# Recurrence sums by accumulating DMAs in place of adds, with three buffers and per-step preparation

## The reference

```
tf    = sigmoid(sum(cond))                       # per batch
decay = exp(-exp(w)) * (0.5 + 0.5 * tf)          # per batch and channel
ek, ekv = exp(min(k, 30)), exp(min(k, 30)) * v   # v = k here
nf, df = forward scans of a = a*decay + ekv, b = b*decay + ek     # over time
nb, db = the same scans backwards
euk = exp(min(u + k, 30))
num = nf + nb - ekv + euk * v
den = df + db - ek + euk
gate = sigmoid(x) * num / max(den, 1e-8) * (0.8 + 0.2 * tf)
```

## Time and profile before

| | |
|---|---|
| median of 3 runs | 501.41 us (500.61 to 501.68) |
| span of the profiled execution | 502.5 us |
| VectorE busy | 336.9 us, 67% |
| TensorE busy | 286.8 us, 57% |
| ScalarE busy | 186.0 us, 37% |
| GpSimd busy | 135.9 us, 27% |
| share of the chain that ended last | VectorE 38%, TensorE 34%, issue 9%, GpSimd 8%, ScalarE 8% |
| data moved by DMA | 7.53 MB |

### The profile page before, as it was taken

The page is one execution under the profiler, slowest core; times in us unless marked ns, Lnnn a source line. Parts: engine busy times, 40 slices in busy tenths (PEclk is TensorE's granted clock), DMA queues, the critical chain, the costliest instruction groups (busy, mean ns, idle before and its releaser), DMA issues.

```text
span 502.5 us, 5307 instructions
## 1 busy us (share of the span) xinstructions
PE 286.8 (57%) x1958; PEld 179.4 (36%) x1958; DVE 336.9 (67%) x533; ACT 186.0 (37%) x272; POOL 135.9 (27%) x122
## 2 busy tenths in 40 slices
PE   0031055325475525237245776889899999964753
PEld 0021032112233213113123335576677777732532
DVE  1998999798979889999446665424443533069553
ACT  6521153733463432344132213252463442325322
POOL 2545452565435462654510210200100000000000
PEclk9999999976556677656666876886956575596887
DMA  7000000000002000000400000000000000000010
GB/s 239 1 0 1 0 0 1 1 0 2 0 1 85 0 0 1 0 0 1 168 1 0 0 1 0 1 1 2 0 1 1 2 0 1 1 0 1 22 42 21
DMA packets 4056, 7.53 MB, mean 15 GB/s; under 512 B 1088, under 2 KB 2496, under 8 KB 3648
## 3 DMA queue, kind: packets, MB, share of 16 engines
q1 hardware_dynamic: 4032, 7.21, 4.2%
HBM read 6.16 MB, written 1.05 MB: 14 GB/s over the span
## 4 chain that ended last, share of the span: by engine, by line
DVE 38%; PE 34%; issue 9%; POOL 8%; ACT 8%; DMA 1%; SPq 1%; DVEq 0%; ACTq 0%; POOLq 0%
PE PS L1107 9%; DVE db L627 6%; PE PM L1056 5%; PE PO L1124 4%; DVE df L627 3%; DVE nb L627 3%; PE PM L953 3%; DVE nf L627 3%; DVE rsum L695 3%; POOL df L281 3%; PE PM L1005 3%; POOL df L282 3%; DVE EU L863 2%; PE PO L988 2%; ACT E L467 2%
## 5 line engine op out<-in xcount | busy, mean ns | idle before, releaser
L797 DVE TENSOR_REDUCE kp<-PS 128x2 f32<-128x256 f32 x64 | 32.2, 553 | 37.6 <-PE PS L1087 37.5
L980 PE MATMUL PO<-E,vt 128*32 128x256 f32 x256 | 30.6, 626 | 38.4 <-DVE ytok L722 24.8
L988 PE MATMUL PO<-ident,yc 128*128 128x128 f32 x64 | 20.3, 416 | 56.3 <-ACT yc L452 56.3
L385 ACT ACTIVATE df<-df,lnmin 128x512 f32<-128x512 f32 x16 | 11.5, 720 | 101.3 <-POOL df L282 101.3
L538 ACT ACTIVATE E<-PS 128x384 f32<-128x384 f32 x64 | 29.7, 491 | 46.2 <-PE PS L1107 45.5
L467 ACT ACTIVATE E<-PS,negc,escale 128x1024 f32<-128x1024 f32 x32 | 38.3, 1197 | 22.6 <-PE PS L967 22.6
L695 DVE TENSOR_REDUCE rsum<-E 128x4 f32<-128x1024 f32 x32 | 38.1, 1207 | 1.4 <-ACT E L467 1.4
L281 POOL TENSOR_TENSOR df<-df,db 128x512 f32<-128x512 f32 x16 | 24.9, 1557 | 51.7 <-DVE nb L627 51.6
L279 POOL TENSOR_TENSOR mv<-EU,vf 128x512 f32<-128x512 f32 x12 | 25.0, 2082 | 42.7 <-DVE EU L617 42.7
L627 DVE TENSOR_TENSOR_SCAN db<-DT,ek 128x512 f32<-128x512 f32 x16 | 34.5, 2158 | 0.0
L941 PE MATMUL PM<-w,sg 128*128 128x256 f32 x32 | 14.7, 637 | 33.2 <-DVE sg L637 33.2
(11 more groups left out here) (160 smaller groups left out, 652.1 us busy)
## 6 DMA issues: line engine op xcount, KB each, us to landing
kT<-in_kT SPq DMA_DIRECT2D x4, 256.0 KB, 4.3
xT<-in_xT SPq DMA_DIRECT2D x4, 256.0 KB, 5.9
G<-in_attn SPq DMA_DIRECT2D x1, 1024.0 KB, 4.9
ek<-in_w SPq DMA_DIRECT2D x1, 1024.0 KB, 4.9
ekv<-in_w SPq DMA_DIRECT2D x1, 1024.0 KB, 7.0
out<-G SPq DMA_DIRECT2D x8, 128.0 KB, 1.7
w<-in_attn SPq DMA_DIRECT2D x1, 512.0 KB, 7.1
cond<-in_cond SPq DMA_DIRECT2D x1, 128.0 KB, 4.4
```

Source lines behind the costliest of these rows:

```text
L797: nc.vector.tensor_reduce(kp[:, b % 2, u * H + 2 * j:u * H + 2 * j + 2, D], PS[:, at0:at0 + 2, lo:hi], AX, ALU.max, negate=True).then_inc( ...
L980: ins = nc.tensor.matmul(PO[SLOT * g:SLOT * (g + 1), q % 2, 0:T], vt[:, b % 2, v * H + 4 * c + g, :], E[:, (2 * q + g // 2) % 4, g % 2, v ...
L988: ins = nc.tensor.transpose(PO[:, q % 2, T + u * P:T + (u + 1) * P], yc[:, q % 2, u * P:(u + 1) * P], ident[:])
```

## The change

VectorE's four scans write to `fwd[r]` and `bwd[r]`, each a tile of two rows of 512 (denominator and numerator side by side), the two forward scans first. ScalarE writes exp(u+k) of one step to `mid[r][0]`, VectorE turns it into m there, GpSimd writes m*v to `mid[r][1]`. Two DMAs on GpSimd's queue with `accum_op=ALU.add` then add 128 x 1,024 floats each: `mid` onto `fwd` when the forward scans are done, and, when that has landed and the backward scans are done, `bwd` onto `fwd`. GpSimd waits for the first; the second's landing is waited for by ScalarE. The adds L281, L282, L284, L285, L597 and L599 go. The rings have three places.

`eu(l)` and `decay_wide(l)` become `prepare(n)`: two exponentials of 256 columns and one copy of 2 x 255 decays per step, the segment borders being zeroed once at the start. `prepare(n+1)` stands behind the reciprocal of step n. Tiles that the second half of the program borrowed from the old buffers are moved to others.

```diff
-        RING = 2
-        mv = sb("mv", [P, RING, SEG])
-        nf = sb("nf", [P, RING, SEG])
...
+        RING = 3
+        DT = [sb(f"DT{i}", [P, SEG + 8]) for i in range(2)]
+        mid = sb("mid", [P, RING, 2, SEG])
+        fwd = sb("fwd", [P, RING, 2, SEG])
+        bwd = sb("bwd", [P, RING, 2, SEG])
...
 # GpSimd
             def wkv(n):
                 l, b, r = wkv_at(n)
-                m = EU[l % 2][:, seg(b)]
+                turns = 16 * (n // RING + 1)
                 pool.wait_ge(S["m_done"], n + 1)
-                if n >= RING:
-                    pool.wait_ge(S["gate_ready"], n + 1 - RING)
-                if n < B:
-                    nc.gpsimd.tensor_tensor(mv[:, r], m, vf[:, seg(b)], ALU.mult).then_inc(S["mv_done"], 1)
-                else:
-                    link(nc.gpsimd.tensor_tensor(mv[:, r], m, vf[:, seg(b)], ALU.mult))
-                pool.wait_ge(S["scan_done"], 4 * (n + 1))
-                link(nc.gpsimd.tensor_tensor(df[:, r], df[:, r], db[:, r], ALU.add))
-                nc.gpsimd.tensor_tensor(df[:, r], df[:, r], m, ALU.add).then_inc(S["den_ready"], 1)
-                if n >= B:
-                    link(nc.gpsimd.tensor_tensor(nf[:, r], nf[:, r], nb[:, r], ALU.add))
-                    nc.gpsimd.tensor_tensor(nf[:, r], nf[:, r], mv[:, r], ALU.add).then_inc(S["num_ready"], 1)
+                nc.gpsimd.tensor_tensor(mid[:, r, 1], mid[:, r, 0], vf[:, seg(b)], ALU.mult).then_inc(S["mv_done"], 1)
+                pool.wait_ge(S["mv_done"], n + 1)
+                pool.wait_ge(S["scan_done"], 4 * n + 2)
+                nc.gpsimd.dma_start(fwd[:, r], mid[:, r], accum_op=ALU.add).then_inc(S[f"mid_added{r}"], 16)
+                pool.wait_ge(S[f"mid_added{r}"], turns)
+                pool.wait_ge(S["scan_done"], 4 * n + 4)
+                nc.gpsimd.dma_start(fwd[:, r], bwd[:, r], accum_op=ALU.add).then_inc(S[f"back_added{r}"], 16)
...
 # ScalarE
-            def eu(l):
-                if l >= 2:
-                    act.wait_ge(S["den_ready"], B * (l - 1))
+            def prepare(n):
+
+                l, b, r = wkv_at(n)
+                if n >= RING:
+                    act.wait_ge(S[f"mid_added{r}"], 16 * (n // RING))
                 for h in range(HALF):
-                    nc.scalar.activation(halves(EU[l % 2])[:, :, h, :], halves(kT)[:, :, h, :], ACT.Exp,
-                                         bias=vec[:, 1, l, h:h + 1]).then_inc(S["eu_done"], 1)
+                    nc.scalar.activation(mid[:, r, 0, h * T:(h + 1) * T], kT[:, seg(b, h * T, T)], ACT.Exp,
+                                         bias=vec[:, 1, l, h:h + 1]).then_inc(S["prep_done"], 1)
+                if n == 0:
+                    act.wait_ge(S["decay_ready"], 1 + LAYERS)
+                if n >= 2:
+                    act.wait_ge(S["scan_done"], 4 * (n - 1))
+                nc.scalar.activation(DT[n % 2][:, 0:SEG].rearrange("p (h t) -> p h t", t=T)[:, :, 1:T],
+                                     dec[:, l, b, :, None].broadcast_to([P, HALF, T - 1]),
+                                     ACT.Copy).then_inc(S["prep_done"], 1)
...
                 if 2 <= p < B * PAIRS + 2 and wkv_slot(p - 2) >= 0:
                     wkv(wkv_step(p - 2))
+                    if wkv_step(p - 2) + 1 < LAYERS * B:
+                        prepare(wkv_step(p - 2) + 1)
...
-                if p == 5:
-                    eu(2)
-                if p == 12:
-                    decay_wide(3)
-                if p == 14:
-                    eu(3)
...
 # VectorE
             def gate(n):
-                if n < B:
-                    link(nc.vector.tensor_tensor(nf[:, r], nf[:, r], nb[:, r], ALU.add))
-                    dve.wait_ge(S["mv_done"], n + 1)
-                    link(nc.vector.tensor_tensor(nf[:, r], nf[:, r], mv[:, r], ALU.add))
-                else:
-                    dve.wait_ge(S["num_ready"], n + 1 - B)
                 dve.wait_ge(S["rec_done"], n + 1)
...
-                dve.wait_ge(S["eu_done"], HALF * (l + 1))
+                dve.wait_ge(S["prep_done"], 3 * (n + 1))
...
+                for i, src in enumerate((ek, ekv)):
+                    nc.vector.tensor_tensor_scan(fwd[:, r, i], ahead, src[:, seg(b)], 0.0, ALU.mult,
+                                                 ALU.add).then_inc(S["scan_done"], 1)
+                for i, src in enumerate((ek, ekv)):
+                    nc.vector.tensor_tensor_scan(bwd[:, r, i][:, ::-1], behind, src[:, seg(b)][:, ::-1], 0.0, ALU.mult,
+                                                 ALU.add).then_inc(S["scan_done"], 1)
```

More of the change, by code:

```diff
@@ L87, in build @@
         G = [sb(f"G{l}", [P, N]) for l in range(LAYERS)]
-        EU = [sb(f"EU{i}", [P, N]) for i in range(2)]
-        DT = [sb(f"DT{i}", [P, N + 8]) for i in range(2)]
-        RING = 2
-        mv = sb("mv", [P, RING, SEG])
-        nf = sb("nf", [P, RING, SEG])
-        nb = sb("nb", [P, RING, SEG])
-        df = sb("df", [P, RING, SEG])
-        db = sb("db", [P, RING, SEG])
+        RING = 3
[3 more added lines that the diff above has]
+        bwd = sb("bwd", [P, RING, 2, SEG])
+        halfs = sb("halfs", [P, 2 * CH * T])
         vec = sb("vec", [P, 2, LAYERS, HALF])
@@ L170, in build @@
         x3tok = [G[2][:, i * SEG:(i + 1) * SEG].rearrange("p (u c) -> p u c", u=TT) for i in range(B)]
[L171 to L173 removed]
+        xrnd = [fwd[:, 0, i, :].rearrange("p (u c) -> p u c", u=TT) for i in range(2)]
+        xqb = [mid[:, 0, i, 0:SEG // 2].bitcast(BF16).rearrange("p (u c) -> p u c", u=TT) for i in range(2)]
+        xqT = [bwd[:, 0, i // 2, (i % 2) * SEG // 2:(i % 2 + 1) * SEG // 2].bitcast(BF16)
                .rearrange("p (u k t) -> p u k t", u=TT, k=HALF) for i in range(B)]
[L175 to L176 removed]
+        hrelu = [fwd[:, 1 + i].rearrange("p n c -> p (n c)") for i in range(2)]
+        hsq = [bwd[:, 1 + i].rearrange("p n c -> p (n c)") for i in range(2)]
         hqb = [kT[:, i * HID // 2:(i + 1) * HID // 2].bitcast(BF16) for i in range(2)]
@@ L297, in _ @@
             nc.gpsimd.memset(epsc[:], EPS_RMS).then_inc(S["pads_set"], 1)
+            for i in range(2):
+                nc.gpsimd.memset(DT[i][:, 0:SEG + 1:T], 0.0).then_inc(S["decay_edge"], 1)
             pool.wait_ge(S["cond_tanh"], 1)
@@ L310, in _ @@
             wkv(1)
-            decay_zero(1)
             wkv(2)
@@ L389, in decay_wide @@
[L389 to L395, removed]
+                nc.scalar.activation(fwd[:, r, 0], fwd[:, r, 0], ACT.Exp, scale=-1.0).then_inc(S["rec_done"], 1)
@@ L406, in _ @@
                     nc.scalar.activation(cth[:], csum[:], ACT.Tanh, scale=0.5).then_inc(S["cond_tanh"], 1)
-            decay_wide(0)
-            eu(0)
+            act.wait_ge(S["decay_edge"], 2)
+            prepare(0)
+            prepare(1)
             for b in range(B):
@@ L412, in _ @@
             act.wait_ge(S["ln_bias"], 1)
+            prepare(2)
             wkv(0)
-            decay_wide(1)
-            eu(1)
+            prepare(3)
             def rms(b):
@@ L458, in _ @@
             kT_copy(0)
+            prepare(4)
             for p in range(SLOTS0):
@@ L620, in wkv @@
                     dve.wait_ge(S["gate_ready"], n + 1 - RING)
-                dve.wait_ge(S["decay_tile"], l + 1)
                 dve.wait_ge(S["ekv_done"], b + 1)
-                fwd = DT[l % 2][:, seg(b)]
-                bwd = DT[l % 2][:, seg(b, 1)][:, ::-1]
-                for out, src, back in ((df, ek, False), (db, ek, True), (nf, ekv, False), (nb, ekv, True)):
-                    s = src[:, seg(b)]
-                    nc.vector.tensor_tensor_scan(out[:, r][:, ::-1] if back else out[:, r], bwd if back else fwd,
-                                                 s[:, ::-1] if back else s, 0.0, ALU.mult,
+                ahead = DT[n % 2][:, 0:SEG]
+                behind = DT[n % 2][:, 1:SEG + 1][:, ::-1]
+                for i, src in enumerate((ek, ekv)):
[3 more added lines that the diff above has]
+                    nc.vector.tensor_tensor_scan(bwd[:, r, i][:, ::-1], behind, src[:, seg(b)][:, ::-1], 0.0, ALU.mult,
                                                  ALU.add).then_inc(S["scan_done"], 1)
```

39 lines of the change are left out of this document (15 added, 24 removed).

## The result

The changed kernel takes 559.95 us (median of 4 runs, 557.99 to 561.94), the kernel before 501.01 (median of 4, the three runs given above and one more). The ratio is 1.1165, 95% interval 1.1102 to 1.1227: 59 us slower. The forecast was 550, in a range of 504 to 590.

What follows compares the result with a forecast made beforehand. Bound: ScalarE's in-order stream waiting for the denominator, in the first half. Terms 44.0 - 1.5 + 9.9 - 10.8 + 3.2 + 4.0 = +48.8 on 501.4 gave 550 us, range 504 to 590.

Steps and rivals of the forecast that it cites:

- The signs that were named: Sums near 14 us after L617 starts; L385 waiting over 10 us for a DMA; L617 intervals 21.7, 23.9 and 16.2.
- slot 0: First of eight slots in a recurrence period; steps stand at slots 0, 3 and 6; its L617 interval forecast at 16.2 us.
- The unknown, L = 4.9: One accumulating DMA from issue to landing, 4.9 us, taken from the 1,024 KB load row; 3.6 to 6.2 got 0.60.
- a plain copy's price: Rival: each DMA lands in 3.1 us like a plain 512 KB; sum about +3, 504 us; chance 0.13.
- prepare, 1.1 us on the path: ScalarE's two exponentials and decay copy for the next step, behind the denominator: 1.1 us per step.
- the third kind: Intervals from slot 6 to the next slot 0: 12.9 us of VectorE's own work before, 16.2 forecast.
- by columns a quarter: Sizing of ScalarE's per-step preparation: a quarter of a layer's cost, 1.0 us, taken as 1.1 with a third instruction.
- The eight intervals, +42.5: Steps 4 to 15, slots 0 to 3 and 3 to 6: 5.5 us more each, 44.0, less 1.5 for layer 0's adds.
- the three, +9.9: Steps 4 to 15, slot 6 to next 0: L617 after 16.2 us against 12.9, 3.3 us more each.
- The first four steps, -10.8: Start to step 4: earlier start, gates without two adds, L613 unslowed (-0.9); step 4 at 52.6, not 63.38.
- The tail: Step 15 to the last gate: gate starts 15.05 us after L617 instead of 11.84, +3.2.
- the shared queues: Two 1,024 KB weight loads beside the last two accumulates, +3; the attention weights' load once, +1.

Runs made afterwards that it cites:

- the kernel with adds: Changed kernel with its two DMAs taken out and the four adds of a step given back to GpSimd, `prepare` still behind the reciprocal: 514.55 us, ratio 1.025.
- the last kernel: Denominator by GpSimd adds, numerator by DMAs, `prepare` ahead, GpSimd's multiply moved behind the denominator's adds, numerator's scans first: 480.89 us, ratio 0.9574 of the kernel before.

## Why the prediction was right

- **What bounds the kernel.** Right: ScalarE's in-order stream behind the denominator, not VectorE's load. VectorE has 25 us less work and the kernel takes 59 us more; taking 1.6 us off each landing gave 39.6 back. The signs that were named came: sums at m+13.9, the steps of slot 0 released by the decay copy L369, intervals of 22.2 and 24.2 for the 21.7 and 23.9 forecast.
- **The unknown, L = 4.9, by the bytes read.** Measured 4.5 from the issue's record, and 0.5 us from the release to that record, so 5.0 in the sum. The choice of the row with as many bytes read came within 0.4 us, and the copy's 2.9 shows that it mattered: with a plain copy's price I would have said 504. That the bytes read are the reason isn't shown. The row was a load from outside SBUF on another queue, so some luck is in how near it came. The prediction put GpSimd's issue inside L, and there it is.
- **prepare, 1.1 us on the path.** Measured 1.35 to 1.4 in each interval; 11.7 us in all in the kernel with adds, and beside the DMAs it chained the third kind to the landing. With it ahead of the reciprocal, the third kind is 6 us shorter. Mis-sized by 0.3 us per step, the term "by columns a quarter": two short exponentials take 0.89 us together.
- **The eight intervals, +42.5; the three, +9.9.** Measured +46.8 and +13.8. The difference is 0.2 us of sums and 0.3 of preparation for each, and the kernel before took 12.3 us in the mean of the third kind, not 12.9, which I had read off one of three. The one landing beside the attention weights took 5.3 us for 4.5, near the +1 forecast for it.
- **The first four steps, -10.8.** Measured -8.7. From L597 at 28.32 to the end of L604 at 32.31 is 4.0 us, not 3.9, which changes little. Step 0 started at 10.03, not 9.5, the k load having landed a microsecond later; the memset started at 38.38 instead of 37.5 and took 2.13 us; and L613 of step 3 was still slowed, by the v rows and not by an add, so its -0.9 didn't come.
- **The tail.** +3.2 and +3 for the shared queues; measured +8.1. The collision was foreseen and costed 1.6 us low: the last landing grew by 4.1 us and the one before by 0.5.
- **The sum.** +48.8 forecast, +60.0 to the last gate, +58.9 in the medians. Each term had its sign. All were off the same way, most by a few tenths, eleven times over, so nothing cancelled.
- **What I didn't say.** The DMAs have a real gain, 8.0 us in the first four steps, and 12.2 us to the last gate where the numerator alone uses them (232.3 against 244.5 with adds). The prediction booked it under dropped adds, as a gain of VectorE's; with the adds given to GpSimd instead, step 4 comes 0.7 us sooner than before, though step 0 starts 2.1 us sooner.

## What to carry to other kernels

Before a sum is moved to a DMA, ask who waits for it and how long after: a landing of 3 to 5 us is free where the consumer comes 7 to 15 us later, as the gate did here, and costs its whole length in every round where an in-order engine stands behind it. Split the work by that, put whatever an engine can do while it waits ahead of the wait in its stream, and keep GpSimd's two-input instructions away from VectorE's, reductions excepted. A change that removes busy time from the busiest engine and lengthens a chain of waits has to be judged by the chain.

## What the runs showed of the hardware

- An accumulating DMA from GpSimd inside SBUF, 128 rows: 4.5 us for 512 KB, 3.3 for 256 KB; a plain one 2.9 for 512 KB. The issue holds GpSimd 0.87 us (copy 0.59), and its record starts 0.5 us after the scan that releases it, where a GpSimd add starts 0.13 after.
- Two loads of 1,024 KB beside it stretch a landing from 4.56 to 8.65 us, and the landing of the second load from 6.9 to 10.0.
- A VectorE instruction with two SBUF inputs beside a GpSimd one with two took 1.0 us longer in each case here: a scan 2.22 for 1.2, the product ekv 1.64 for 0.69, one of 128 columns 1.31 for 0.29. Of instructions with one input, TENSOR_SCALAR was slowed alike (ek 1.37 for 0.43) and the row sums were not, beside the same adds (1.17 to 1.22). The Trainium skill (SBUF — State Buffer, section Who interferes with whom) names such pairs as contending; these are the amounts. The records look like taking turns: in step 15 of the changed kernel one scan ends at 286.20, GpSimd's multiply, begun beside it, at 287.26, and the next scan, begun beside that, at 288.33, about 1.1 us apart.
- A DMA issued by GpSimd beside a scan didn't slow it: in every step of the last kernel the scans stay at 1.2 us.
